# A decoder layer on one core: softmax in pairs of heads, with one exponential and one causal mask per pair

## The reference

```python
scores = (jnp.einsum('bhsd,bhtd->bhst', q, k) + bias) / math.sqrt(HD)
scores = 30.0 * jnp.tanh(scores / 30.0)
scores = jnp.where(causal[None, None], scores, -jnp.inf)
ctx = jnp.einsum('bhst,bhtd->bhsd', jax.nn.softmax(scores, axis=-1), v)
x = x + ctx @ Wo.T + bo
x = x + cross_attention(layernorm(x), ctx_2048, mask)
x = x + down(silu(gate(layernorm(x))) * up(layernorm(x)))
```

## Time and profile before

| | us |
|---|---|
| median of three runs | 579.44 |
| lowest, highest run | 578.35, 582.94 |
| profiled execution | 580.64 |
| its span in the trace | 578.9 |

### The profile page before, as it was taken

One profiled execution on the slowest core, in us unless ns is written; L12 is line 12 of the kernel. 1 busy time (PEld: TensorE's weight loads), 2 busy tenths in 40 slices (PEclk: granted clock), 3 DMA queues, 4 the chain that ended last, 5 costly groups with the idle time before them and its releaser, 6 DMA issues.

```text
span 578.9 us, 9934 instructions
## 1 busy us (share of the span) xinstructions
PE 551.5 (95%) x3890; PEld 452.1 (78%) x3890; DVE 339.7 (59%) x674; ACT 243.2 (42%) x471; POOL 279.8 (48%) x284
## 2 busy tenths in 40 slices
PE   2998998999989999899999999999999999999997
PEld 2787876888768887687887787888888888888885
DVE  6478737975488754986767674345533564233322
ACT  3537882668626676237753242023311333023310
POOL 5756769855667666888767230023400343013310
PEclk9999999999999999899999999999999999999999
DMA  8861223441215420194181902100001000100001
GB/s 263 301 200 43 71 75 108 129 165 41 88 57 145 148 66 27 55 308 135 56 307 41 303 0 92 54 19 1 1 31 43 1 0 1 44 30 0 2 18 54
DMA packets 44189, 50.98 MB, mean 88 GB/s; under 512 B 3184, under 2 KB 25712, under 8 KB 44144
## 3 DMA queue, kind: packets, MB, share of 16 engines
q1 hardware_dynamic: 44144, 50.36, 26.9%
HBM read 36.72 MB, written 13.63 MB: 87 GB/s over the span
## 4 chain that ended last, share of the span: by engine, by line
PE 80%; POOL 7%; DVE 6%; ACT 4%; issue 1%; DMA 1%; SPq 0%; DVEq 0%; ACTq 0%
PE bank L262 52%; PE bank L398 15%; PE bank L257 3%; PE bank L336 2%; PE bank L318 2%; PE bank L354 2%; PE bank L343 2%; POOL probs L638 2%; DVE q_m L1058 1%; DVE q_m L1060 1%; POOL x_res L659 1%; PE bank L310 1%; POOL rstd L627 1%; POOL q_w L647 1%; POOL q_w L645 1%
## 5 line engine op out<-in xcount | busy, mean ns | idle before, releaser
L262 PE MATMUL bank<-reduced 128*128 128x512 f32 x1536 | 363.0, 395 | 1.6 <-DVE reduced L988 1.6
L262 PEld LDWEIGHTS bank<-reduced 128*128 128x128 f32 x1536 | 287.6, 189 | 64.4 <-issue 3.3
L742 POOL TENSOR_TENSOR f_parts<-fused,f_parts 128x512 fp32r<-128x512 f32 x48 | 62.2, 1295 | 174.8 <-ACT f_parts L929 174.8
L911 ACT ACTIVATE tanh_g<-bank,half_gate 128x512 f32<-128x512 f32 x48 | 33.1, 689 | 152.5 <-PE bank L262 152.3
L398 PE MATMUL bank<-reduced,f_parts 128*128 128x512 f32 x384 | 89.0, 391 | 0.0
L398 PEld LDWEIGHTS bank<-reduced,f_parts 128*128 128x128 f32 x384 | 71.8, 188 | 15.6 <-issue 0.8
L638 POOL TENSOR_SCALAR_AFFINE_SELECT probs<-probs 128x512 f32<-128x512 f32 x64 | 41.6, 681 | 61.8 <-ACT probs L794 61.8
L1174 DVE SCALAR_TENSOR_TENSOR silu<-tanh_g,bank 128x512 f32<-128x512 f32 x48 | 32.9, 686 | 57.4 <-ACT tanh_g L911 57.4
L789 ACT ACTIVATE probs<-bank 128x512 f32<-128x512 f32 x64 | 33.0, 602 | 50.1 <-PE bank L318 47.4
L645 POOL TENSOR_TENSOR q_w<-q_w,q_m 128x512 f32<-128x512 f32 x36 | 46.9, 1302 | 4.2 <-DVE q_m L1060 4.2
L647 POOL TENSOR_TENSOR q_w<-q_w,q_m 128x512 f32<-128x512 f32 x36 | 47.2, 1312 | 2.8
(11 more groups left out here) (86 smaller groups left out, 536.2 us busy)
## 6 DMA issues: line engine op xcount, KB each, us to landing
quantized<-q_w SPq DMA_DIRECT2D x36, 256.0 KB, 3.3
reduced<-quantized SPq DMA_DIRECT2D x12, 512.0 KB, 7.5
memT_sb<-in_memT SPq DMA_DIRECT2D x16, 256.0 KB, 4.7
mem_sb<-in_mem SPq DMA_DIRECT2D x16, 256.0 KB, 5.5
out<-y_sb SPq DMA_DIRECT2D x16, 256.0 KB, 2.0
x_res<-in_x SPq DMA_DIRECT2D x3, 1024.0 KB, 7.0
q_w<-in_gate_w SPq DMA_DIRECT2D x12, 256.0 KB, 3.2
q_w<-in_up_w SPq DMA_DIRECT2D x12, 256.0 KB, 3.3
```

The costliest lines, as they stand in the source:

```text
L262: ins = pe.matmul(dst, stationary, moving, start=(n == 0), stop=(n == len(pairs) - 1))
L742: pool.tensor_tensor(f_lo[:, f, :], fused[:, f % 2, :], f_hi[:, f, :].bitcast(F32), ALU.subtract).then_inc(f_lo_ready, 1)
```

## The change

The softmax goes two heads at a time. On ACT a new helper `heads(g, hg, j)` issues tanh of head j, tanh of head j + 1, and one exp over both (128 x 1024). Each stage has two of these in a row at its head. `q_out` now stands behind the second pair in every stage, and `k_out` behind it with no exp between; `cross`, `context_high` and (at the FFN's start) `gate(0, 0)` that stood between exps stand behind the second pair as well. In (g, 2) `q_out` and `context_high` change places. On POOL `causal` masks two heads with one affine_select over 128 x 1024, and waits for the exp of the pair. The semaphores `exped` and `masked` count two for each stage instead of four, and PE's wait in `context` counts so too. DVE, SP and the order on PE are unchanged.

```diff
-                pe.wait_ge(masked, (m + 1) * 4)
+                pe.wait_ge(masked, (m + 1) * 2)
...
             def causal(g, hg):
-                for j in range(4):
-                    pool.wait_ge(exped, (g * HG + hg) * 4 + j + 1)
-                    pool.affine_select(out=probs[:, j], in_=probs[:, j], compare_op=ALU.is_ge, fill=0.0,
-                                       base=0, pattern=[[0, GT], [1, S]], channel_multiplier=-1).then_inc(masked, 1)
+
+                for j in range(0, 4, 2):
+                    pool.wait_ge(exped, (g * HG + hg) * 2 + j // 2 + 1)
+                    two = probs[:, j:j + 2].rearrange("p j i s -> p (j i) s")
+                    pool.affine_select(out=two, in_=two, compare_op=ALU.is_ge, fill=0.0,
+                                       base=0, pattern=[[0, 2 * GT], [1, S]], channel_multiplier=-1).then_inc(masked, 1)
...
             def exp(g, hg, j):
+
                 wait_drained(act, ("S", g, hg, j))
-                act.activation(probs[:, j], probs[:, j], ACT.Exp, scale=CAP).then_inc(exped, 1)
+                wait_drained(act, ("S", g, hg, j + 1))
+                act.activation(probs[:, j:j + 2], probs[:, j:j + 2], ACT.Exp, scale=CAP).then_inc(exped, 1)
+
+            def heads(g, hg, j):
+                tanh(g, hg, j)
+                tanh(g, hg, j + 1)
+                exp(g, hg, j)
...
-                for j in range(4):
-                    tanh(g, 0, j)
+                heads(g, 0, 0)
+                heads(g, 0, 2)
                 q_out(g, 1)
                 if g >= 2:
                     cross(g - 2, 2)
-                exp(g, 0, 0)
-                exp(g, 0, 1)
                 k_out(g, 1)
                 if g >= 2:
                     cross(g - 2, 3)
-                exp(g, 0, 2)
-                exp(g, 0, 3)
                 if g:
                     context_high(g - 1, 3)
...
-                for j in range(4):
-                    tanh(g, 1, j)
+                heads(g, 1, 0)
+                heads(g, 1, 2)
                 q_out(g, 2)
-                for j in range(4):
-                    exp(g, 1, j)
                 k_out(g, 2)
...
-                for j in range(4):
-                    tanh(g, 2, j)
+                heads(g, 2, 0)
+                heads(g, 2, 2)
+                q_out(g, 3)
                 context_high(g, 1)
-                q_out(g, 3)
-                for j in range(4):
-                    exp(g, 2, j)
                 k_out(g, 3)
...
-                    for j in range(4):
-                        tanh(g, 3, j)
+                    heads(g, 3, 0)
+                    heads(g, 3, 2)
                     q_out(g + 1, 0)
-                    exp(g, 3, 0)
-                    exp(g, 3, 1)
                     if g:
                         cross(g - 1, 0)
-                    exp(g, 3, 2)
-                    exp(g, 3, 3)
                     k_out(g + 1, 0)
...
-            for j in range(4):
-                tanh(G - 1, 3, j)
-            exp(G - 1, 3, 0)
-            exp(G - 1, 3, 1)
+            heads(G - 1, 3, 0)
+            heads(G - 1, 3, 2)
             gate(0, 0)
-            exp(G - 1, 3, 2)
-            exp(G - 1, 3, 3)
             cross(G - 2, 0)
             context_high(G - 1, 2)
```

## The result

| | before | after |
|---|---|---|
| median | 580.12 | 573.43 |
| lowest, highest run | 578.35, 582.94 | 572.44, 573.83 |
| profiled execution | 580.64 | 573.54 |
| its span | 578.9 | 571.8 |

The ratio is 0.9874, 95% interval 0.9840 to 0.9909: 1.3% less time. The forecast was 574.1, or 0.9% less.

The account below looks back on a forecast made before the run. PE bounds the kernel (80% of the last-ending chain), so only its waits can be gained. 1.5 + 1.15 + 0.25 + 1.2 + 0 + 1.2 = 5.3, taken from the median 579.44, gives 574.1, 0.9% less; range 571.6 to 577.6.

Parts of the forecast that it names:

- The prices of a pair: On ACT a merged exp takes 1.05 (bounds 0.95, 1.25); on POOL a merged mask 1.20 (bounds 1.1, 1.36).
- rival D: Merged mask on POOL runs at a poorer rate; at 3.0 per pair 7 lost, 586.8; chance 0.04.
- Rival C: V's evictions and POOL's slab work bound groups 0 and 1; only (3, 2) gains: 578.2; chance 0.06.
- (0, 1) and (0, 3): Stages where PE waits for POOL's last mask: gains 1.5 (bounds 1.2, 1.82) and 1.15 (lower bound 0.7).
- (1, 0): Stage where the chain from K's eviction to V's last eviction moves earlier: gain 1.2, bounds 0.8 and 1.4.
- (2, 0) and (3, 0): Stages where a new 1.1 stall for the fourth tanh is eaten by an old wait: 0 each, bounds +1.1, -0.1.
- rival B: Gain partly turns into other waits: 1.1 stalls pass through (2.2), or rounding holds masks; 576.3, up to 578; chance 0.25.
- (3, 2): Stage where exps fill ACT's idle wait and PE's transpose wait for K's eviction goes: gain 1.2, bounds 0.9, 1.4.
- (0, 0): Stage where V's last eviction would come when PE's product is there: gain 0.25, bounds 0 and 0.3.
- rival A: The low clock stretch behind the idle of (3, 0) may not come: 1.5 more, 572.6; chance 0.22.
- base case: The stage gains, sum 5.3, come as worked out: 572.9 to 575.5, likeliest 574.1; chance 0.43.
- The port: In (0, 1) mask and DVE exclude each other: mask ends 50.8 to 51.4, sum 5.0 to 5.6 instead of 5.3.

Follow-up runs that it names:

- e1: The changed kernel's new order with single exps and single masks, one head at a time; 573.33, ratio 0.9877 to the kernel before.
- e2: The kernel before with merged exps and masks standing in the old order; 583.23, ratio 1.0045 to the kernel before.
- e9: The changed kernel with the old order in stages (g, 0) alone, exps still merged; 578.01, ratio 0.9938 to the kernel before.
- e3: The changed kernel with four tanhs first, then the two merged exps, in front of Q's eviction; 573.14, ratio 0.9875 to the kernel before.
- e5: The changed kernel with four tanhs first in stages (g, 0) alone, pairs elsewhere; 570.74, ratio 0.9831 to the kernel before.
- e7: The changed kernel with every causal mask done twice in a row; 583.33, ratio 1.0042 to the kernel before.
- e8: The changed kernel with four tanhs first in (g, 0), and V's evictions first on DVE in groups 1 and 2 only; 569.32, ratio 0.9805.
- e6: The changed kernel with four tanhs first in (g, 0) and V's evictions first on DVE; 571.44, ratio 0.9835 to the kernel before.
- e4: The changed kernel with DVE's last slab preparations of (g, 0) put behind V's last eviction and the cross attention; 574.02, ratio 0.9892.

## Why the prediction was right

**The reading.** That the exps stood behind Q's eviction and this behind PE's product, and that this order and not the arithmetic is what matters, is shown by e1 (order alone: the whole gain) and e2 (merging alone: 0.45% slower). That PE's waits came from there and nowhere else is shown for the stages (g, 0) by e9; for (0, 1), (0, 3) and (3, 2) it rests on the waits that are gone, in the changed kernel as in e1.

**The prices of a pair.** The groups by form of the kernel after:
```profile
L798 ACT ACTIVATE probs<-probs 128x1024 f32<-128x1024 f32 x32 | 34.0, 1062 | 2.9
```
```profile
L640 POOL TENSOR_SCALAR_AFFINE_SELECT probs<-probs 128x1024 f32<-128x1024 f32 x32 | 36.6, 1147 | 35.5 <-ACT probs L798 35.3
```
1.06 for 1.05, and 1.15 for 1.20 (1.10 undisturbed). Interpolating between two forms of the same operation was good to 5%. With this rival D, the dear mask, was out. Rival C, that only (3, 2) gains, is out by the gains of (0, 1), (0, 3) and (1, 0).

**(0, 1) and (0, 3).** Gains 1.75 and 1.16 for 1.5 and 1.15. The first term was too small because I let DVE's normalisation stretch the second mask by 0.3, as it stretched the single ones. It took 1.12, unstretched; DVE paid instead (2.77 for its four normalisations, 2.23 before), and nobody waited for it.

**(1, 0).** Gain 1.39 for 1.2. The chain after, beside the earlier trace rows: K's eviction and the high part on ACT, the low part on POOL, V's eviction on DVE:
```profile
78.42 0.69 ACT L783 ACTIVATE kT<-bank,bk_c 128x512 f32<-128x512 f32 x1 [0.40 <-PE bank L262]
79.01 0.62 ACT L810 ACTIVATE reduced<-ctxT 128x512 fp32r<-128x512 f32 x1
```
```profile
79.72 1.29 POOL L632 TENSOR_TENSOR reduced<-ctxT,reduced 128x512 fp32r<-128x512 f32 x1 [1.11 <-ACT reduced L810]
```
```profile
90.78 0.68 DVE L987 TENSOR_TENSOR v<-bank,bv_b 128x512 f32<-128x512 f32 x1
```
From K's eviction to the low part it is 1.30 instead of 2.50, as worked out. e9, with the old order in (g, 0), gives it back.

**(2, 0) and (3, 0).** The balance, 0, was right; its wording, "the new stall is eaten by the old one", was not. ACT and PE of the kernel after, beside the earlier trace rows:
```profile
146.66 0.62 ACT L810 ACTIVATE reduced<-ctxT 128x512 fp32r<-128x512 f32 x1
```
```profile
138.81 0.33 PE L359 MATMUL bank<-identity,x_sc 128*128 128x128 f32 x1 [1.28 <-ACT probs L791]
...
160.35 1.13 PE L354 MATMUL bank<-mem_sb,x_pT 128*128 128x512 f32 x2 [0.99 <-DVE x_res L1031]
```
The wait for DVE did fall by 1.1 as the stall came. But the chain that ends in that wait begins with ACT's high part, behind the same stall: the stall is passed on in full, and what pays for it is the pair of exps that no longer stands in front of the high part. The two happen to be equal. So rival B had this much right, that the stalls pass through; its 2.2 did not come, because the exps pay for them. The prediction had both terms in its sum (-1.04 and +1.1) and drew the wrong picture from them; my expectation for e3 went by the picture. e3 and e5, which take the stall away, gain 1.1 to 1.2 in each stage.

**(3, 2).** Gain 1.42 for 1.2. ACT after, where the earlier trace rows had an idle 1.97 before the high part:
```profile
262.05 0.67 ACT L787 ACTIVATE qT<-bank,bq_c 128x512 f32<-128x512 f32 x1
262.61 0.62 ACT L810 ACTIVATE reduced<-ctxT 128x512 fp32r<-128x512 f32 x1
263.45 0.69 ACT L783 ACTIVATE kT<-bank,bk_c 128x512 f32<-128x512 f32 x1 [0.22 <-PE bank L262]
```
The exps fill the idle time; K's eviction waits for its product and for nothing else.

**(0, 0).** The 0.25 can't be told from the scatter of the start. V's last eviction was to come with PE's product; PE waits 0.60 and 0.34 for it in the two traced executions, so this step isn't borne out.

**The clock, rival A.** The low stretch did not come: the granted clock of the span was 0.999 after. But between the two traced executions it did not give 1.5. (3, 0) is 0.20 shorter. PE and DVE of the kernel before at its end, then PE of the kernel after:
```profile
237.72 1.13 PE L354 MATMUL bank<-mem_sb,x_pT 128*128 128x512 f32 x2 [2.14 <-DVE x_res L1038]
...
242.04 0.74 PE L310 MATMUL bank<-bias_r,bias_l 4*128 4x512 f32 x4
242.61 1.07 PE L318 MATMUL bank<-qT,kT 32*128 32x128 f32 x32
```
```profile
241.19 0.75 DVE L1038 SCALAR_TENSOR_TENSOR x_res<-bank,x_w,x_res 128x512 f32<-128x512 f32 x1
```
```profile
235.21 0.43 PE L336 MATMUL bank<-probs,sums_to 128*32 128x128 f32 x8 [0.38 <-DVE v L987]
236.59 0.50 PE L310 MATMUL bank<-bias_r,bias_l 4*128 4x512 f32 x4 [0.73 <-issue]
```
At full speed PE comes earlier to V's last eviction, and then to the bank of the last read-out, which DVE drains behind a slab, and waits there. In the kernel before DVE drained that bank until 241.94, and PE, at half speed, was there at 242.04. From the start of the read-out's last products (L354) to the next scores (L318) it took 4.89 before and 4.65 after. So nearly all of this slow stretch lay over work that DVE would have made PE wait for anyway, and for this execution 1.5 was too much. e2 and e7 show the other side: where the stretch reaches into the large products of (g, 1) it costs 1.5 to 2.6. The rule of the Trainium skill that I set beside the rival (TensorE: Matmul & The Clock Gate, Part 1), that the gate follows how busy PE has been, would have less idle bring less of the low clock; the traces agree: 0.995 of full speed before, 0.999 after, 1.000 in e8, and 0.987 in e2, which waits more than the kernel before. So do the clocks of the executions above: 0.991 to 0.999 before, 0.999 or 1.000 after. By them the rival was right in kind, and over many executions its 1.5 was too small and not too large: about 2.3 of the difference of the medians go with the clock. The base case, which left the clock out, had 5.3 for the 5.5 that are there at full clock.

**The port.** The rule of the Trainium skill (SBUF — State Buffer, Who interferes with whom), that a two-port VectorE instruction and a GpSimd one exclude each other for a whole instruction, agrees with e3: four normalisations of 0.5 each took 5.09 beside a POOL that never paused, 1.27 each, about the length of one POOL instruction (1.2 to 1.5 there). In (0, 1), where I weighed it, the mask took 1.12, DVE's four normalisations 0.5 more than before, and it cost PE nothing. In (3, 2) of e3 it cost 1.1.

**The chances, and luck.** The sum was 5.3, of which 0.25 in (0, 0) can't be told. Without it the terms add up to 5.05, where the stages show 5.7 (5.9 less the 0.2 of the clock in (3, 0)); each of the large ones was 0 to 0.25 too small. With the median 0.7 under the forecast, and that of the kernel before 0.7 higher over all its runs than it was at first, the time crossed the line of 1%, on whose other side I had the larger chance (0.53). That the time itself came within 0.7 of 574.1 is luck in part. I subtracted from 579.44, the median of three executions; over the 38 others the kernel before has 581.3, and less 5.3 that is 576.0, 2.5 too long, nearly all of it the clock that the base case left out. The low start made up for it.

## What to carry to other kernels

Ask of every instruction in an in-order queue what it waits for, and put those whose inputs are ready in front of those that wait for another engine: that was the whole gain here, and merging the instructions was worth nothing. When a stall and a saving meet in one chain, check whether the later wait has its own source or starts behind the stall; only in the first case is the stall hidden. A slow clock or a long wait may lie over other waits that are only a little shorter: ask what is late next before counting either as gain. One traced execution can't say how often the slow clock comes: compare the granted clocks of many.

## What the runs showed of the hardware

- A merged exp over 1024 elements took 1.06, the next instruction could start 0.97 after it, and two single ones are 1.04 apart. Waiting for the end of the second tanh costs 0.20: the exp starts 0.68 behind that tanh's start, where an instruction that need not wait for it starts 0.48 behind. Of this, 0.06 lie behind a semaphore instruction that carries the second wait and that e1 has not. From one pair's first tanh to the next pair's it is 2.14, and 2.01 in e1 with two single exps (medians over the stages). So the merged exp saved ACT nothing.
- The affine_select goes linearly, 0.29, 0.64 and 1.10 for 128, 512 and 1024 elements.
- Back-to-back work on POOL holds up DVE's normalisations (`tensor_scalar`, 128 x 512): four of them took 1.9, 2.2 to 2.8, 4.1 and 5.1 as POOL's pauses closed, and 5.5 in (3, 1) of e6.
- The half clock (a granted clock of 0.50, 1.2 GHz) came behind waits of PE of 1.93, 2.14, 2.40, 2.42, 2.42, 2.43 and 2.48 (in e2, before, e2, e7, e9, e9, e2), and did not behind others of 2.13, 2.19, 2.40 and 2.48 (before, before, e2, e9). It came behind shorter waits too where several stood near each other: 1.59 and 0.44 in (3, 2) of e6, 1.06, 1.49 and 0.96 in (3, 0) of e7, 1.59, 0.44 and 1.77 in (3, 2) of e4. The longest wait alone does not tell. In the traces of the changed kernel, e1, e3, e5 and e8, whose waits in the attention are 1.3 and less, no such stretch was seen there. A stretch cost between 0 and 2.6, by what PE had to do in it.
